# A two-layer graph attention kernel: fold of W1 over two pairs of PSUM banks, a window ring of two banks, score rows in pieces, and W1 loaded and split earlier

## The reference

```python
def _gat_layer(x, src, dst, W, a_src, a_dst, bias, concat):
    h = (x @ W).reshape(N, H, C)
    al_s = jnp.einsum('nhc,hc->nh', h, a_src)
    al_d = jnp.einsum('nhc,hc->nh', h, a_dst)
    e = leaky_relu(al_s[src] + al_d[dst], 0.2)
    m = segment_max(e, dst)
    ex = exp(e - m[dst])
    alpha = ex / (segment_sum(ex, dst)[dst] + 1e-16)
    out = segment_sum(h[src] * alpha[:, :, None], dst)
    return (out if concat else out.mean(axis=1)) + bias
h = elu(_gat_layer(x, src, dst, W1, as1, ad1, b1, concat=True))    # 4 heads of 512
out = _gat_layer(h, src, dst, W2, as2, ad2, b2, concat=False)      # 1 head of 768
x = _layernorm(x + out)
```

## Time and profile before

| | |
|---|---|
| median of 3 runs (range) | 955.25 us (954.58 to 955.36) |
| profiled execution, its own time | 957.13 us |
| its span | 955.3 us, of which 1.83 us lie around it |
| PE busy | 887.2 us, 93% |
| DVE, ACT, POOL busy | 64%, 44%, 23% |
| mean granted clock of PE | 0.977 |
| DMA moved | 111.19 MB, mean 116 GB/s |

### The profile page before, as it was taken

The page is one execution under the profiler, slowest core; times in us unless marked ns, Lnnn a source line. Parts: engine busy times, 40 slices in busy tenths (PEclk is TensorE's granted clock), DMA queues, the critical chain, the costliest instruction groups (busy, mean ns, idle before and its releaser), DMA issues.

```text
span 955.3 us, 15152 instructions
## 1 busy us (share of the span) xinstructions
PE 887.2 (93%) x5719; PEld 800.6 (84%) x5719; DVE 606.9 (64%) x1155; ACT 424.1 (44%) x686; POOL 223.3 (23%) x148
## 2 busy tenths in 40 slices
PE   4997885999999999999999998989999999699996
PEld 2455553889888998889988897989999999699996
DVE  9547743658893698828887388663222344397887
ACT  5346433257643675437663385852111111387300
POOL 1000003035321243122431266500000000154452
PEclk9999897999999999999999999999999999889999
DMA  8508994553467334582164333446232441400223
GB/s 299 134 1 119 151 169 134 137 151 132 158 193 189 121 115 139 170 202 95 38 193 117 103 132 121 135 142 150 54 84 47 78 75 30 98 3 2 59 88 97
DMA packets 64451, 111.19 MB, mean 116 GB/s; under 512 B 31772, under 2 KB 33464, under 8 KB 63004
## 3 DMA queue, kind: packets, MB, share of 16 engines
q1 hardware_dynamic: 64379, 110.22, 45.1%
HBM read 85.25 MB, written 24.94 MB: 115 GB/s over the span
## 4 chain that ended last, share of the span: by engine, by line
PE 65%; DVE 12%; issue 8%; POOL 6%; ACT 3%; SPq 3%; DMA 2%; DVEq 1%; POOLq 0%; ACTq 0%
PE ps L1683 19%; PE ps L1685 18%; PE ps L1684 18%; POOL pbuf L586 5%; PE ps L1714 3%; PE ps L1655 2%; DVE pbuf L599 2%; PE ps L1804 2%; SPq L656 2%; PE ps L1645 1%; DVE h2f L1594 1%; DMA w1raw<-in_L_gnn_W 1%; DVE h2f L1568 1%; DVE ring L1338 1%; DVE vbuf L1413 1%
## 5 line engine op out<-in xcount | busy, mean ns | idle before, releaser
L586 POOL TENSOR_TENSOR pbuf<-pbuf,grow 125x625 f32<-125x625 f32 x100 | 170.4, 1704 | 549.0 <-ACT pbuf L571 248.8
L1683 PE MATMUL ps<-hx,PThi 125*125 125x260 f32 (+5 forms) x800 | 228.2, 285 | 6.7 <-DVE vbuf L1407 3.8
L1685 PE MATMUL ps<-hx,PTlo 125*125 125x260 f32 (+5 forms) x800 | 225.9, 282 | 0.0
L1684 PE MATMUL ps<-hlo,PThi 125*125 125x260 f32 (+4 forms) x800 | 225.6, 282 | 0.0
L1683 PEld LDWEIGHTS ps<-hx,PThi 125*125 125x125 f32 x800 | 149.4, 187 | 11.3 <-DVE PTlo L613 3.5
L1684 PEld LDWEIGHTS ps<-hlo,PThi 125*125 125x125 f32 x800 | 149.8, 187 | 1.5
L1685 PEld LDWEIGHTS ps<-hx,PTlo 125*125 125x125 f32 x800 | 149.7, 187 | 0.0
L599 DVE SCALAR_TENSOR_TENSOR pbuf<-pbuf,counts 125x625 f32<-125x625 f32 x100 | 98.6, 986 | 25.3 <-ACT pbuf L593 25.1
L1683 PE MATMUL ps<-W2p,hT 128*125 128x384 f32 x320 | 109.7, 343 | 3.2 <-DVE hT L1419 1.7
L608 ACT ACTIVATE PThi<-pbuf 125x625 fp32r<-125x625 f32 x80 | 57.8, 723 | 114.4 <-DVE pbuf L599 57.5
L1685 PE MATMUL ps<-W2p,hT 128*125 128x384 f32 x320 | 108.1, 338 | 0.0
(11 more groups left out here) (187 smaller groups left out, 1611.4 us busy)
## 6 DMA issues: line engine op xcount, KB each, us to landing
xr<-xT_scratch SPq DMA_DIRECT2D x30, 750.0 KB, 4.7
nbm<-mask_scratch SPq DMA_DIRECT2D x40, 273.4 KB
hidden_scratch<-vbuf SPq DMA_DIRECT2D x40, 224.0 KB
hblk<-hidden_scratch SPq DMA_DIRECT2D x10, 896.0 KB
xT_scratch<-xa SPq DMA_DIRECT2D x20, 375.0 KB, 11.5
w1f<-in_L_gnn_W SPq DMA_DIRECT2D x12, 512.0 KB, 9.3
w1raw<-in_L_gnn_W SPq DMA_DIRECT2D x4, 1536.0 KB, 7.9
w2raw<-in_L_gnn_W SPq DMA_DIRECT2D x14, 384.0 KB, 5.1
```

The lines of the kernel that those rows point to most:

```text
L586: pool.tensor_tensor(pslot(c), pslot(c), src[:, g * GN:(g + 1) * GN], ALU.add).then_inc(e_done, 1)
L1683: pe.matmul(dst, ahi, bhi, start=start, stop=False, skip_group_check=shared)
L1684: pe.matmul(dst[:, 0:n], ahi, blo, start=False, stop=False, skip_group_check=shared)
L1685: return pe.matmul(dst, alo, bhi, start=False, stop=stop, skip_group_check=shared)
```

## The change

In words, by engine:

- WRING goes from 3 to 2: the windows use banks 0 and 1. Bank 2 takes half of the fold's product and later the score rows. The transposes of the fold go in turn to banks 3, 4 and 5, 6 (`fold_banks`), so that step i waits for the copy of step i - 2, not i - 1. Each product still has 384 moving columns.
- FS goes from 8 to 10: two more fold steps ahead of the windows, and the fold ends in window 6, not 8.
- The first increment of `oh_free`, which lets DVE begin its one-hots, comes from the first transposes of the program, not from window 0.
- Masks begin three windows earlier (CT 8 to 5), x two windows earlier (XW 11 to 9).
- The score rows come in pieces (`row_steps`): two of the six k in each of windows 14 to 19, the last third whole in window 20; their columns for `al` in window 21 instead of 24.
- ACT makes `W1hi` in windows 24 to 26, DVE makes `W1lo` in windows 25 to 27 in place of POOL.
- SP loads W1 after five of the ten stores of x instead of after all; five pairs are stored later, between the mask stores and loads. ACT now waits for all of them before it overwrites `xa` with the first chunk.

```diff
-WRING = 3
+WRING = 2
-XW = 11
-FS = 8
+XW = 9
+FS = 10
-CT = 8
-WSPL = 26
-WROW = 21
+CT = 5
+WSPL = 24
+WROW = 14
...
+        def row_bank(c):
+            return PS[0:2 * H, WRING, 0:(TCH[c][1] - TCH[c][0]) * B]
+        def row_steps(w):
+            u = w - WROW
+            if 0 <= u < 6:
+                return u // 3, range(2 * (u % 3), 2 * (u % 3) + 2)
+            return (2, range(KD)) if u == 6 else (None, ())
+        def fold_banks(i):
+            return PS[:, 3 + 2 * (i % 2):5 + 2 * (i % 2), 0:DH]
...
             store_nb(0)
-            for j in range(NB):
+            store_xT(0)
+            store_xT(1)
+            store_nb(1)
+            store_xT(2)
+            store_xT(3)
+            store_nb(2)
+            store_xT(4)
+            store_nb(3)
+            sp.wait_ge(xt_lo, NB)
             load_w1(0)
-            store_nb(5)
+            store_xT(5)
+            store_nb(4)
...
             load_srow(0)
+            store_xT(6)
+            store_nb(5)
             for b in range(MR - 1):
                 load_nb(0, b)
+            store_xT(7)
             store_nb(6)
+            store_xT(8)
             store_nb(7)
+            store_xT(9)
+            store_nb(8)
...
-            for k in range(KD):
-                split_w1(0, k)
...
+            act.wait_ge(xT_stored, 32 * NB)
             act_hi(act, 0)
...
+                if w > WSPL and w <= WSPL + 3:
+                    split_w1(0, 2 * (w - WSPL) - 2)
+                    split_w1(0, 2 * (w - WSPL) - 1)
...
+            t.then_inc(oh_free, 1)
...
-                    if i >= 1:
-                        pe.wait_ge(wt_sb, i)
+                    if i == 1:
+                        pe.wait_ge(plan, 8)
+                    if i >= 2:
+                        pe.wait_ge(wt_sb, i - 1)
...
+                for i in folds(w):
+                    fold_step(i)
                 if w >= CT and (w - CT) % 3 == 0:
                     transpose_counts((w - CT) // 3)
-                for i in folds(w):
-                    fold_step(i)
...
-                if WROW <= w < WROW + 3:
-                    score_rows(w - WROW)
-                if w == WROW + 3:
+                if row_steps(w)[1]:
+                    score_rows(*row_steps(w))
+                if w == WROW + 7:
```

More of the change, by code:

```diff
@@ L650, in store_nb, with store_xT @@
                     sp.dma_start(nb_d[b, lo:hi, :], nbs[b % 2][lo:hi, :]).then_inc(nb_stored[b % 2], 16)
-            store_nb(0)
-            for j in range(NB):
+            def store_xT(j):
                 sp.wait_ge(xt_lo, j + 1)
@@ L1017, in weights_out @@
                 act.wait_ge(wt_ps, u + 1)
-                act.activation(wT[:, u % 2, :].rearrange("p (a k) -> p a k", a=2), PS[:, 3:5, 0:DH], ACT.Copy).then_inc(wt_sb, 1)
+                act.activation(wT[:, u % 2, :].rearrange("p (a k) -> p a k", a=2), fold_banks(u), ACT.Copy).then_inc(wt_sb, 1)
             def folded_rows_out():
                 act.wait_ge(wrow_ps, 1)
-                act.activation(warow[:, 0:DH], PS[0:2 * H, 5, 0:DH], ACT.Copy)
+                act.activation(warow[:, 0:DH], PS[0:2 * H, WRING, 0:DH], ACT.Copy)
                 act.activation(warow[:, DH:D], PS[0:2 * H, 7, 0:DH], ACT.Copy).then_inc(wrow_sb, 1)
@@ L1029, in score_rows_out @@
                 act.activation(rows[:, TCH[c][0] * B:TCH[c][1] * B],
-                               PS[0:2 * H, 6 + c % 2, 0:(TCH[c][1] - TCH[c][0]) * B], ACT.Copy).then_inc(rows_sb, 1)
+                               row_bank(c), ACT.Copy).then_inc(rows_sb, 1)
             act.wait_ge(consts, 8)
@@ L1056, in _ @@
                     mask_out((w - CT) // 3)
-                if WROW < w <= WROW + 3:
-                    score_rows_out(w - WROW - 1)
+                if KD - 1 in row_steps(w)[1]:
+                    score_rows_out(row_steps(w)[0])
                 if WSPL <= w < WSPL + 3:
@@ L1073, in _ @@
             for j in range(NB - 2):
-                if j in (1, 2):
-                    mask_out(NB - 3 + j)
+                if j == 1:
+                    mask_out(NB - 1)
                 split_h(j)
@@ L1641, in fold_step @@
                         pe.wait_ge(ld_wf[i // (FU // 2)], 16 * KD)
-                    if i >= 1:
-                        pe.wait_ge(wt_sb, i)
+                    if i == 1:
+                        pe.wait_ge(plan, 8)
+                    if i >= 2:
+                        pe.wait_ge(wt_sb, i - 1)
                     for k in range(KD):
-                        t = pe.transpose(PS[:, 3 + k // 3, k % 3 * 128:(k % 3 + 1) * 128],
+                        t = pe.transpose(fold_banks(i)[:, k // 3, k % 3 * 128:(k % 3 + 1) * 128],
                                          w1f[:, i // 4, k, i % 4 * 128:(i % 4 + 1) * 128], ident[:, :])
@@ L1728, in transpose_counts, with score_rows @@
                 t.then_inc(ct_ps, 1)
-            def score_rows(c):
+            def score_rows(c, ks):
                 lo, hi = TCH[c]
-                if c == 0:
-                    pe.wait_ge(xt_lo, NB)
-                if c == 2:
-                    pe.wait_ge(rows_sb, 1)
-                for k in range(KD):
-                    t = products(PS[0:2 * H, 6 + c % 2, 0:(hi - lo) * B],
+                if ks[0] == 0:
+                    pe.wait_ge(xt_lo, hi)
+                    if c == 0:
+                        pe.wait_ge(wrow_sb, 1)
+                    else:
+                        pe.wait_ge(rows_sb, c)
+                for k in ks:
+                    t = products(row_bank(c),
                                  ((wahi[:, k, :], walo[:, k, :]), (xa[:, 0, k, lo:hi, :].rearrange("p b n -> p (b n)"),
@@ L1741, in score_rows @@
                                  k == 0, k == KD - 1)
-                t.then_inc(rows_ps, 1)
+                if ks[-1] == KD - 1:
+                    t.then_inc(rows_ps, 1)
             def spread(col, place, lo=0, hi=NB):
@@ L1785, in _ @@
                 h_block(j)
-                if j < 2:
-                    transpose_counts(NB - 2 + j)
+                if j == 0:
+                    transpose_counts(NB - 1)
             pe.wait_ge(nbs_done, NB)
```

13 lines of the change are left out of this document (3 added, 10 removed).

## The result

The changed kernel takes **947.0 us** (median of 5 runs, 945.8 to 948.5) against 954.6 for the kernel before on the same chip (5 runs, 952.7 to 955.4): ratio 0.9924, 95% interval 0.991 to 0.994. It is 0.8% faster; 1.6% was forecast. The profiled execution took 947.9 us by its own time, its span 946.1, so against that of before it is 9.2 us shorter. The broadcast of the first shift is 9.4 us earlier than in the earlier trace rows, so the whole difference arises ahead of it; the chunks behind it take what they took (PE busy 48.27 of 50 us, against 48.26 in the earlier trace rows).

The account below looks back on a forecast made before the run. PE is nearly full from 195 us on, so the change pays only by starting that part earlier: -17.4 us at the broadcast plus 2.0 for DMA gives -15.4, a median of 940.0 us, range 934 to 947.

Parts of the forecast that it names:

- the hole's cure: PE busy only 3.9 of 16.9 us from 142 to 159; closing this brings the first h block 16.8 us earlier.
- Step 3, the x phase: Windows 9 to 21: 3.67 us per window to window 17, window 21 done at 117.1 us, before at 133.6.
- step 4: the loads of the plan: Windows 22 to 29, done at 140.7 us: 1.0 us allowed for one plan among the windows where DVE splits W1.
- Step 7, DMA: SP's new queue order: W1 wait gone, but ACT waits for a late mask store, taking back 2.0 us.
- Step 3, the row matmuls: Windows 14 to 17: six score-row matmuls each, 1.4 us, fill PE's waiting time since the x loop takes 3.67 anyway.
- Step 1, the fold: Start of the windows: two more fold steps cost 4.4 us, a 0.9 wait goes; window 0 at 37.0, window 1 at 42.9.
- Step 2: Windows 1 to 8, summed window by window, end at 69.4 us with x already in window 8.
- Step 4, the split on DVE: Three windows after window 25: DVE makes two parts of `W1lo` in each, charged 4.1 us with no cover.
- Step 5, the clock: Window 29, counts and first products: PE's clock may fall to half, costing 1.3 us, bounds 0 and 3.
- Step 6: The h blocks take 36.1 us as before, less 0.6 for a transpose of counts: -17.4 us at the broadcast.
- The ring of two: All windows: waiting for the copy of window w - 2 costs nothing; upper bound 0.62 us in each window.
- B: SP's queue: masks stand behind stores of x, ACT waits 6.32 us again; 944.3 us, or 948.6 with late loads; chance 0.17.

Follow-up runs that it names:

- Without the stores: Changed kernel with all ten stores of x moved behind the mask loads, read only to the first h block: 140.12 us against 150.5 in the changed kernel.
- the swap: Changed kernel with W1's low part made on POOL, as before the change, instead of DVE: ratio 0.9935 to the kernel before; 0.988 with two windows per load.

## Why the prediction was wrong

The forecast was 940.0 us, -15.4 by the profile's own time; it came to -9.2, and the median of 947.0 just misses the range's end of 947. The direction and the hole's cure were right. What failed, by the prediction's steps:

- **Step 3, the x phase, and step 4: the loads of the plan.** They had 1.2 us for one load (window 20) and 1.0 for another (window 28), from the single row at 81.07 in the earlier trace rows. Five loads show, with 9.7 us of waits (1.5 of them perhaps the copies'), 7.5 more than counted, and stretches at the lower clock stand behind three of them. This is the term that was mis-sized. The trace of the kernel before has four such waits (1.20, 0.69, 0.69 and 0.61 us), not one. Without the stores the program followed the sum: window 14 at 86.9 (87.8 forecast), 18 at 104.0 (103.0), 20 at 109.8 (108.8), 22 at 117.1 (117.1), 29 at 137.6 (137.8), first h block at 140.1 (142.0). With them it is late by 3.2 at window 14, 5.4 at 18, 5.8 at 22, 9.3 at 29, 8.5 at the first h block.
- **Step 7, DMA.** It asked of SP's stores which buffer comes free late, and found 2.0 us at ACT. No such wait came. The stores cost 10.4 us at the first h block, through the loads.
- **Step 3, the row matmuls.** "It fills the time in which PE waited" was half true: 0.8 of 1.4 us a window lengthen the loop, 3.2 us in four windows (17.38 against 14.17). In the run without stores, shorter windows elsewhere made up for it (windows 20 and 21 took 7.3 us, 8.3 were forecast), so its agreement with the sum is in part luck.
- **Step 1, the fold,** held: window 0 at 37.5 (37.0), window 1 at 43.4 (42.9). **Step 2:** window 9 starts at 71.0, 1.6 behind the 69.4 of the forecast, 1.0 of which is the wait at window 8.
- **Step 4, the split on DVE,** was charged 4.1; its three pairs take 3.9, and PE waits 3.5 us for one-hots in windows 26 to 28. That POOL would cost as much is shown by the swap. **Step 5, the clock,** gave window 29 and what follows 1.3, and its matmuls do lose 1.2 (2.58 us in place of 1.41). But the clock falls behind loads too, which was not counted: window 12 loses 1.1 (2.48), and windows 24 and 28 lose 1.3 each (2.71). **Step 6** held: the broadcast is 35.3 us behind the first h block (36.4 before).
- **The ring of two** was taken as nothing, and is (1.0003). The Trainium skill (Perfetto Trace Analysis, Matmul Optimizations) wants all banks in play for instructions in flight. The runs here don't bear out that a shorter window ring costs: the ratio is 1.0003, and in the kernel after, at most the 1.5 us at windows 8 and 28 can be the shorter ring's.

Of the rivals, B named the right suspect, the stores of x in SP's queue, and a time of 944.3 to 948.6 that holds the result, but its mechanism (masks late, ACT waiting) shows in no row of the kernel after, so it was not right either. The row that could have given it was there: 1.20 us "issue" before a matmul that had all it needed, at a window number divisible by four. The prediction took the duration and did not ask what the engine did in it, whether it would come back at every load, and what shared its way.

Shown: the loads stand on the path, and their price has a part by the value and a part that the stores of x add. Nearly shown: the stores act through the loads, since with none left they cost nothing, though waits of another kind could hide a share there. Argued only: why one window per load loses just 3.1 us to the stores although it has the most loads; short ones may fit into the time in which PE still works off what was issued, which the trace cannot show. Argued too: that the growing sum is what slows the windows of the single load. Open: what in the stores of x lengthens a load, and why the same loads waited so much less in the kernel before.

## What to carry to other kernels

A load of loop counts or addresses into an engine's registers is work on the engine's own path, and shows only as "issue". Before such a kernel is filled up with other work, look for waits that come back with the period of these loads. Load few values at a time, here for one or two windows (0.5 to 0.6%, 5 to 6 us, beside the 7.6 that the whole change brought). All at once lost here for two reasons, and only one is the load: look also at what the program must work out from the values in each step, and store running sums ready made rather than let each step add them up.

When a hole is closed, small waits ahead of it that cost nothing can begin to cost: two windows per load gave 0.6% after the change and nothing before it. And ask of a DMA queue not only which buffer its transfers free late, but what else goes slower beside them.

## What the runs showed of the hardware

- Eight more values in a register load cost 1.9 to 2.0 us of waiting on the mean (12.1 and 11.1 us in six loads), 0.24 us each, with or without the stores of x; a load of 31 values at the start took at most 7.6 us, 0.24 each as well.
- With stores of x in the DMA queues such a load waits longer: 2.52 in place of 0.29 us, 2.82 in place of 0.34. In six loads of 13 values the stores added 7.8 us, in six windows with loads of 5 values 6.8. Beside the load of W1 (DMA share 0.99, 382 GB/s) a load of 13 values waited 2.13 us, no more than the 2.62 where the share was 0.37.
- Work with registers shows as "issue" on the engine that does it: with the plan of all windows in one load, DVE stood 2.1 to 2.5 us at "issue" ahead of the one-hots of windows 23, 24, 25 and 28, and PE waited 19.4 us for one-hots in place of 4.2.
- In the kernel after PE stood 2.82 us ahead of window 24 at a granted clock of 1.00; behind it the clock was 0.50 from 129.4 to 132.4, and seven matmuls took 2.71 us in place of 1.42.
- POOL's split (1.25 us for a 128x512 tile) beside DVE's one-hots stretches 14 of them from 3.5 to 7.54 us while four tiles are made.
